# Loads in two holds, identity products, repacked FFN weights and a new order of the work, in a fused attention and FFN layer

## The chip, the cores and the metric

One core of one Trainium2 chip. The metric is the device time of an execution in microseconds. The core has five engines with instruction queues of their own, each in order: TensorE (PE in the profile; its weight loads are PEld), VectorE (DVE), ScalarE (ACT), GpSimd (POOL) and SyncE (SP, which here only issues DMAs). They meet through semaphores. Everything is float32, except three helper tiles of the quantisation.

## The reference

For 2048 tokens of width 128, one layer of retention attention and one FFN, each with a residual and a LayerNorm without weights:

```python
q = (hidden_states @ Wq).reshape(b, l, NH, DQK)      # NH = 8, DQK = 16
k = (hidden_states @ Wk).reshape(b, l, NH, DQK)
v = (hidden_states @ Wv).reshape(b, l, NH, DV)       # DV = 32
q = rope(q)
k = rope(k)
...
scores = jnp.einsum('bhqd,bhkd,hqk->bhqk', q * DQK ** (-0.5), k, decay)
o = jnp.einsum('bhqk,bhkd->bhqd', scores, v)
o = jnp.transpose(o, (0, 2, 1, 3))
o = o * jax.lax.rsqrt(jnp.mean(o * o, axis=-1, keepdims=True) + EPS) * g_norm_w
g = hidden_states @ Wg
o = o.reshape(b, l, VDIM) * (g * jax.nn.sigmoid(g))
return o @ Wo
...
gate = fp4_linear(x, w_gate)                         # 128 -> 352
y = fp4_linear(x, w_up)
h = jax.nn.silu(gate) * y
return fp4_linear(h, w_down)                         # 352 -> 128
...
x = _layernorm(x + attention(x))
x = _layernorm(x + ffn(x))
```

`fp4_linear` rounds both the activations and the weights, in blocks of 16 along the contracted axis, to the 8 magnitudes of FP4 times the block's largest magnitude over 6. The decay is causal and exponential in the distance, so the attention can be carried from chunk to chunk as a state.

## The kernel before, in words

The tokens are cut into 16 chunks of 128. For a chunk c the kernel computes, in this order of dependence:

- TensorE project_qk, then VectorE rotate (three products with tables of cosines and sines) and GpSimd rotate_add; TensorE transpose_qk; ScalarE q_even, q_odd and k_transposed (kT);
- TensorE project_vg, ScalarE v_sb and silu_g (copy_v_and_silu);
- TensorE scores, four banks of PSUM. VectorE masks the two heads of the first bank (mask_scores); ScalarE copies the other six (raw) and GpSimd masks them;
- TensorE from_state, state_product and values; VectorE next_state, which carries the state S; ScalarE copy_oT, TensorE transpose_o, ScalarE squares, VectorE mean_square (ms) and gated, GpSimd rms_rstd (rstd_h) and gated_output (y), TensorE transpose_y, ScalarE copy_yT, TensorE out_projection;
- VectorE ln1_sum, ln1_stats, ln1_aggr, ln1_eps; GpSimd ln1_rstd; ScalarE ln1_centre and ln1_norm, which writes x1 (x_blocks in the profile);
- the activation's rounding: VectorE x_amax, x_inv, x_ratio, ScalarE magic_x, VectorE x_plus, x_grid, GpSimd x_value; TensorE transpose_xq, ScalarE copy_xqT, TensorE gate and up, ScalarE silu_of_gate, VectorE h_product;
- the same rounding of the 352-wide h (h_amax to h_value), TensorE transpose_h, ScalarE copy_hT, TensorE down; VectorE ln2_sum, ln2_stats, ln2_aggr, ln2_eps, GpSimd ln2_rstd, ScalarE ln2_norm, and a store of 64 KB by SP.

Each engine's queue is a loop over stages s, written out by hand. In a stage, `run(f, a)` issues operation f of chunk s + a if there is such a chunk. The lists of these lines, one for each engine, and their numbers a set the whole order; nothing else schedules. A "stage" of the prediction is one turn of TensorE's loop. The eight banks of PSUM have several users each (scores, oT, o and yT in banks 0 to 3; QK and its transposes in 4; VG and the output projection in 5; gate, xqT and hT in 6; up, down and the state product U in 7), and TensorE waits for the last user's reader before it fills a bank again.

Before they can be used, the FFN's weights are rounded too, once, on VectorE and ScalarE between the first chunks (weights_amax, weights_inv, weights_ratio, weights_magic, weights_plus, weights_grid, weights_value; number 0 is gate and up, wgu, number 1 is down, wd). TensorE transposes them in stages 2 and 3. `scale_wo` folds the norm's weight into Wo.

Chunks are loaded in groups (chunk 0; 1 and 2; 3 to 7; 8 to 15), each as x transposed, tables and x for the residual. SP issues all loads one after the other, without a wait, and then the 16 stores, each behind a wait for its ln2_norm. ScalarE issues w_vg, the masks and the three other weights before its first work.

## Time and profile before

| | us |
|---|---|
| median of 3 runs | 147.26 (146.16 to 148.52) |
| the profiled execution | 146.5 |
| its span, first to last instruction | 144.8 |
| TensorE busy | 118.7 (82%) |
| VectorE busy | 115.6 (80%) |
| ScalarE busy | 96.0 (66%) |
| GpSimd busy | 101.6 (70%) |

Busy shares are means over the span, in which stages with different limits follow each other; the views by stretch below tell more. Times inside the profile count from the span's start. An instruction's duration in the profile overlaps the next one's start a little when the queue is full. A wait is put down to the engine or DMA that came last.

### The profile page before, as it was taken

The numbers are of one execution on the slowest core, as the hardware profiler recorded it, in microseconds if no ns is written. First come the engines' busy times: TensorE is split into PE (matmuls) and PEld (weight loads), VectorE is DVE, ScalarE is ACT, GpSimd is POOL, SyncE is SP. The second block draws the span as 40 slices with busy tenths as digits, with TensorE's granted clock in tenths as the row PEclk, the third lists the DMA queues.
The fourth block names the chain that finished last, engine by engine and source line by source line (L and its number), as shares of the span: only waits on it lengthen the run. The fifth ranks groups of instructions, "written<-read, shape, count | busy, mean of one in ns | idle before, by whom it ended". The sixth has DMA issues, their size and how long they took to land.

```text
span 144.8 us, 3493 instructions
## 1 busy us (share of the span) xinstructions
PE 118.7 (82%) x1206; PEld 74.1 (51%) x1206; DVE 115.6 (80%) x438; ACT 96.0 (66%) x279; POOL 101.6 (70%) x139
## 2 busy tenths in 40 slices
PE   0339779889999999999999999999999787767600
PEld 0123344636666465675756676666667453435400
DVE  1086979497589999989898989899899999979420
ACT  1316647697877977969595868787788575533680
POOL 4010494786978899879797979898989877464830
PEclk9999999999999999999999999999999999999985
DMA  3999960000000000000000000000000000000143
GB/s 115 243 382 374 440 194 0 0 2 7 0 0 5 0 0 7 0 2 5 0 0 5 0 2 0 5 2 5 0 0 5 0 0 0 2 0 0 37 146 109
DMA packets 6404, 7.57 MB, mean 52 GB/s; under 512 B 667, under 2 KB 5531, under 8 KB 6259
## 3 DMA queue, kind: packets, MB, share of 16 engines
q1 hardware_dynamic: 5712, 6.42, 13.1%
q10 hardware_dynamic: 675, 0.94, 2.1%
q8 instruction: 9, 0.15, 0.4%
q14 instruction: 8, 0.07, 0.2%
HBM read 6.31 MB, written 1.05 MB: 51 GB/s over the span
## 4 chain that ended last, share of the span: by engine, by line
PE 67%; DVE 10%; ACT 6%; POOL 6%; DMA 4%; issue 2%; SPq 1%; ACTq 0%
PE ps L319 9%; PE ps L336 6%; PE ps L460 6%; PE ps L437 6%; PE ps L444 5%; PE ps L376 5%; PE ps L312 5%; DMA tabs<-rope_tables 4%; PE ps L451 4%; PE ps L366 4%; PE ps L400 3%; PE ps L349 2%; PE ps L401 2%; POOL rstd_h L872 2%; ACT x L490 2%
## 5 line engine op out<-in xcount | busy, mean ns | idle before, releaser
L872 POOL TENSOR_TENSOR rstd_h<-ms,minus_half 128x8 f32<-128x8 f32 x16 | 26.3, 1645 | 8.6 <-DVE ms L726 8.2
L883 POOL TENSOR_TENSOR rstd<-veps,minus_half 128x1 f32<-128x1 f32 x32 | 18.7, 594 | 2.1 <-DVE veps L742 2.0
L319 PE MATMUL ps<-w_vg,xT 128*128 128x512 f32 x32 | 18.0, 646 | 0.1
L460 PE MATMUL ps<-wd_T,hT 128*128 128x128 f32 x96 | 14.1, 283 | 4.3 <-DVE h_blocks L779 2.3
L867 POOL TENSOR_SCALAR_AFFINE_SELECT probs<-raw 128x768 f32<-128x768 f32 x16 | 13.9, 866 | 5.1 <-ACT raw L489 4.9
L863 POOL TENSOR_TENSOR qk<-rope_c,rope_s 128x256 f32<-128x256 f32 x16 | 11.7, 730 | 6.4 <-DVE rope_s L703 6.4
L460 PEld LDWEIGHTS ps<-wd_T,hT 128*128 128x128 f32 x96 | 12.5, 191 | 7.2 <-DVE h_blocks L779 4.2
L890 POOL TENSOR_TENSOR xq<-x_grid,xs 128x128 f32<-128x128 f32 x16 | 9.1, 571 | 9.6 <-DVE x_grid L642 9.6
L312 PE MATMUL ps<-w_qk,xT 128*128 128x256 f32 x32 | 11.8, 453 | 4.8 <-DMA w_qk<-in_w_qk 4.8
L896 POOL TENSOR_TENSOR hq<-h_grid,hs 128x352 f32<-128x352 f32 x16 | 12.9, 809 | 3.7 <-DVE h_grid L642 3.7
L489 ACT ACTIVATE raw<-ps 128x768 f32<-128x768 f32 x16 | 13.1, 816 | 1.0 <-PE ps L336 0.8
L490 ACT ACTIVATE q_eo<-ps,consts 128x128 f32<-128x128 f32 x32 | 9.9, 365 | 5.7 <-PE ps L328 5.7
L565 ACT ACTIVATE silu_h<-ps 128x352 f32<-128x352 f32 x16 | 7.4, 463 | 7.9 <-PE ps L437 7.7
L489 ACT ACTIVATE oT<-ps 128x256 f32<-128x256 f32 x16 | 6.2, 384 | 9.5 <-PE ps L376 9.5
L701 DVE TENSOR_TENSOR rope_c<-ps,tabs 128x256 f32<-128x256 f32 x16 | 6.7, 419 | 7.0 <-DMA tabs<-rope_tables 6.4
L336 PE MATMUL ps<-q_eo,kT 32*128 32x256 f32 x128 | 12.1, 444 | 0.2 <-ACT kT L490 0.2
L444 PE MATMUL ps<-wgu_T,xqT 128*128 128x352 f32 x32 | 12.1, 460 | 0.0
L437 PE MATMUL ps<-wgu_T,xqT 128*128 128x352 f32 x32 | 12.1, 460 | 0.0
L489 ACT ACTIVATE hT<-ps 128x384 f32<-128x384 f32 x16 | 7.9, 496 | 4.9 <-PE ps L451 4.8
L877 POOL TENSOR_TENSOR y<-gate_o,rstd_h 128x256 f32<-128x256 f32 x16 | 9.9, 617 | 1.3
L376 PE MATMUL ps<-probs,v_sb 128*32 128x128 f32 x256 | 10.4, 273 | 0.4 <-POOL probs L867 0.4
L451 PE MATMUL ps<-ident,hq 128*128 128x128 f32 x48 | 8.7, 290 | 2.0 <-ACT silu_h L565 1.8
(99 smaller groups left out, 337.4 us busy)
## 6 DMA issues: line engine op xcount, KB each, us to landing
tabs<-rope_tables SPq DMA_DIRECT2D x1, 1536.0 KB, 12.3
out<-x SPq DMA_DIRECT2D x16, 64.0 KB, 1.6
tabs<-rope_tables SPq DMA_DIRECT2D x1, 960.0 KB, 8.7
xT<-x_transposed SPq DMA_DIRECT2D x1, 512.0 KB, 9.3
x_res<-x SPq DMA_DIRECT2D x1, 512.0 KB, 13.4
tabs<-rope_tables SPq DMA_DIRECT2D x1, 384.0 KB, 7.0
wgu_nat<-in_w_gate_up ACTq DMA_DIRECT2D x1, 352.0 KB
xT<-x_transposed SPq DMA_DIRECT2D x1, 320.0 KB, 6.8
```

The costliest lines, as they stand in the source:

```text
L312: mm(qk_ps, xT[:, c * C:(c + 1) * C], w_qk[:], start=True, stop=True).then_inc(qk_pe, 1)
L319: mm(vg_ps, xT[:, c * C:(c + 1) * C], w_vg[:], start=True, stop=True).then_inc(vg_pe, 1)
L336: last = mm(sc_ps(j), kT[rows, c % D, :], q_eo[rows, c % D, :, :].rearrange("p e q -> p (e q)"), start=True, stop=True)
L376: last = mm(oT_ps[32 * slot32:32 * slot32 + 32, n // 4, :], v_sb[:, c % D, n * DV:(n + 1) * DV], probs[:, c % 2, n, :], start=c == 0, stop ...
L437: mm(gate_ps, xqT[:, c % 2, :], wgu_T[:, 0, :], start=True, stop=True).then_inc(gate_pe, 1)
L444: mm(up_ps, xqT[:, c % 2, :], wgu_T[:, 1, :], start=True, stop=True).then_inc(up_pe, 1)
L451: last = transpose(hT_ps[:, t * C:(t + 1) * C], hq[:, c % 2, t * 128:(t + 1) * 128], ident[:])
L460: last = mm(down_ps, hT[:, c % 2, t, :], wd_T[:, t, :], start=t == 0, stop=t == 2)
L489: copy = lambda o, i: nc.scalar.activation(o, i, ACT.Copy)
L867: gp.affine_select(out=probs[:, c % 2, 2 * MB:, :], in_=raw[:, c % 2, :, :], compare_op=ALU.is_ge, fill=0.0, base=0, pattern=[[0, NH - 2 * ...
L872: gp.tensor_tensor(rstd_h[:, c, :], ms[:, c, :], minus_half[:], ALU.pow).then_inc(rms_p, 1)
L883: gp.tensor_tensor(rstd[n][:, c, :], veps[n][:, c, :], minus_half[:, 0:1], ALU.pow).then_inc(ln_p[n], 1)
```

## The change

The tables lose a third: the sines were stored twice, once negated, and the negation is now made by a `scalar_tensor_tensor` in rotate, so a chunk's tables are 128 KB instead of 192 KB. The gate and up weights, 88 rows of 1024 elements before, lie on all 128 partitions with 704 elements each (`WG`), and are loaded by five DMAs instead of one and transposed in other pieces. SP waits after x and tables of chunk 0 until these tables have landed, and again before the last group. w_qk moves from SP to the head of ScalarE's queue, w_down and Wo from ScalarE to SP; the weights of gate and up are issued after ScalarE's first activation. TensorE gets four identity products at its start and four after chunk 0's project_qk. The lists of all four compute engines are written in another order and with other numbers; the loops have 33 stages instead of 38.

```diff
-WR = 88
+WR = I
 WT = I // WR
+WG = 2 * I * H // 128
...
-        FIRST, LAST = -3, 35
+        FIRST, LAST = -4, 29
...
             load_x(0)
-            sp.dma_start(w_qk[:], wqk).then_inc(d_wqk, 16)
             load_tables(0)
+            sp.wait_ge(d_tab[0], 16)
             load_x(1)
             load_tables(1)
+            sp.dma_start(wd_nat[:], w_down).then_inc(d_wd, 16)
+            sp.dma_start(wo_nat[:], wo_g).then_inc(d_wo, 16)
             load_res(0)
             load_res(1)
             load_x(2)
             load_tables(2)
             load_res(2)
+            sp.wait_ge(d_tab[1], 16)
             load_x(3)
             load_tables(3)
             load_res(3)
...
+            def warm_up(n):
+                pe.wait_ge(c_ident, 1)
+                for _ in range(n):
+                    mm(ps[:, 7, 0:C], ident[:], ident[:], start=True, stop=True)
...
                 fill(4, "qk")
+                if c == 0:
+                    warm_up(4)
...
+            act_engine.dma_start(w_qk[:], wqk).then_inc(d_wqk, 16)
             act_engine.dma_start(w_vg[:], wvg).then_inc(d_wvg, 16)
             act_engine.dma_start(consts[:], cst).then_inc(d_cst, 16)
-            act_engine.dma_start(wgu_nat[:], w_gate_up).then_inc(d_wgu, 16)
-            act_engine.dma_start(wd_nat[:], w_down).then_inc(d_wd, 16)
-            act_engine.dma_start(wo_nat[:], wo_g).then_inc(d_wo, 16)
             act.wait_ge(c_pool, 4)
             nc.scalar.activation(table_io[:], minus_half[:], ACT.Silu)
+            act_engine.dma_start(wgu_nat[:, 0:4 * H].rearrange("p (t n) -> p t n", n=2 * H),
+                                 w_gate_up[0:2 * H, :].rearrange("(t p) n -> p t n", p=H)).then_inc(d_wgu, 16)
+            act_engine.dma_start(wgu_nat[0:96, 4 * H:5 * H], w_gate_up[2 * H:I, 0:H]).then_inc(d_wgu, 16)
+            act_engine.dma_start(wgu_nat[96:128, 4 * H:5 * H], w_gate_up[2 * H:288, H:]).then_inc(d_wgu, 16)
+            for m in range(2):
+                act_engine.dma_start(wgu_nat[m * 64:(m + 1) * 64, 5 * H:],
+                                     w_gate_up[288:I, H + m * 64:H + (m + 1) * 64]).then_inc(d_wgu, 16)
...
-                dve.wait_ge((d_wgu, d_wd)[n], 16)
+                dve.wait_ge((d_wgu, d_wd)[n], (80, 16)[n])
...
-                for e in range(2):
-                    vec.tensor_tensor(g16(rope_s[:, c % D, :])[:, :, e, :], g16(qk_ps)[:, :, 1 - e, :],
-                                      g16(tabs[:, c, H:])[:, :, e, :], ALU.mult).then_inc(rope_v, 1)
+                sin = tabs(c)[:, H:].rearrange("p (g f) -> p g f", f=16)
+                vec.scalar_tensor_tensor(g16(rope_s[:, c % D, :])[:, :, 0, :], g16(qk_ps)[:, :, 1, :], -1.0, sin,
+                                         ALU.mult, ALU.mult).then_inc(rope_v, 1)
+                vec.tensor_tensor(g16(rope_s[:, c % D, :])[:, :, 1, :], g16(qk_ps)[:, :, 0, :], sin, ALU.mult).then_inc(
+                    rope_v, 1)
...
-                run(ln2_norm, -19)
...
+                run(ln2_norm, -13)
...
-                run(down, -7)
-                run(gate, -3)
...
+                run(down, -8)
+                run(gate, -4)
```

What the new lists do shows in three places. First, VectorE at the program's start, from behind its memsets (L701, L703 or L726 to L730 rotate, wr_small the weights' maxima and scales, probs the mask). Before:

```order
L701 TENSOR_TENSOR rope_c<-ps,tabs 128x256 [waits qk_pe,d_tab0]
L703 TENSOR_TENSOR rope_s<-ps,tabs 128x8x16 x2
L625 TENSOR_REDUCE wr_small<-wgu_nat 88x64 [waits d_wgu]
L659 TENSOR_SCALAR wr_small<-wr_small 88x64 [waits w0_amax_v]
L661 RECIPROCAL wr_small<-wr_small 88x64 [waits w0_amax_v]
L662 TENSOR_SCALAR wr_small<-wr_small 88x64
L633 SCALAR_TENSOR_TENSOR wr_ratio<-wgu_nat,wr_small 88x1024 [waits w0_inv_v]
L625 TENSOR_REDUCE wr_small<-wd_nat 128x22 [waits d_wd]
L709 TENSOR_TENSOR probs<-ps,causal 128x256 [waits sc_pe,c_ident]
```

and now:

```order
L726 TENSOR_TENSOR rope_c<-ps,tabs_sb 128x256 [waits qk_pe,d_tab0]
L728 SCALAR_TENSOR_TENSOR rope_s<-ps,tabs_sb 128x8x16
L730 TENSOR_TENSOR rope_s<-ps,tabs_sb 128x8x16
L650 TENSOR_REDUCE wr_small<-wgu_nat 128x44 [waits d_wgu]
L650 TENSOR_REDUCE wr_small<-wd_nat 128x22 [waits d_wd]
L684 TENSOR_SCALAR wr_small<-wr_small 128x22 [waits w1_amax_v]
L686 RECIPROCAL wr_small<-wr_small 128x22 [waits w1_amax_v]
L687 TENSOR_SCALAR wr_small<-wr_small 128x22
L736 TENSOR_TENSOR probs<-ps,causal 128x256 [waits sc_pe,c_ident]
L684 TENSOR_SCALAR wr_small<-wr_small 128x44 [waits w0_amax_v]
L686 RECIPROCAL wr_small<-wr_small 128x44 [waits w0_amax_v]
L687 TENSOR_SCALAR wr_small<-wr_small 128x44
```

The large ratio of the gate and up weights has left the stretch ahead of the first mask. Both waits for weight DMAs still stand there, and the DMAs they wait for are issued later.

Second, TensorE in a stage in which every operation has a chunk, from the value products on (L376 or L392 values, L451 transpose_h, L400 and L401 or L416 and L417 out_projection, L384 and L385 or L400 and L401 transpose_o, L444 or L464 up, L319 or L335 project_vg, L429 or L449 transpose_xq, L336 or L352 scores, L457 gate, L480 down). Before:

```order
L376 MATMUL ps<-probs,v_sb 32x128 x8
L451 MATMUL ps<-ident,hq 128x128 x3
L400 MATMUL ps<-wo_s,yT 128x128
L401 MATMUL ps<-wo_s,yT 128x128
L384 MATMUL ps<-ident,oT 128x128
L385 MATMUL ps<-ident,oT 128x128
L327 MATMUL ps<-ident,qk 128x128
L328 MATMUL ps<-ident,qk 128x128
L444 MATMUL ps<-wgu_T,xqT 128x352
L319 MATMUL ps<-w_vg,xT 128x512
L429 MATMUL ps<-ident,xq 128x128
L336 MATMUL ps<-q_eo,kT 128x256 x4
```

and now:

```order
L392 MATMUL ps<-probs,v_sb 32x128 x8
L449 MATMUL ps<-ident,xq 128x128
L416 MATMUL ps<-wo_s,yT 128x128
L417 MATMUL ps<-wo_s,yT 128x128
L400 MATMUL ps<-ident,oT 128x128
L401 MATMUL ps<-ident,oT 128x128
L343 MATMUL ps<-ident,qk 128x128
L344 MATMUL ps<-ident,qk 128x128
L480 MATMUL ps<-wd_T,hT 128x128 x3
L457 MATMUL ps<-wgu_T,xqT 128x352
L335 MATMUL ps<-w_vg,xT_sb 128x512
L352 MATMUL ps<-q_eo,kT 128x256 x4
```

transpose_xq has come ahead of the output projection and transpose_h has left the place; down and gate stand between transpose_qk and project_vg, where up stood alone.

Third, ScalarE at the end of the program (x<-r,rstd is ln2_norm, hT the copy of the transposed h). Before:

```order
L502 ACTIVATE h_magic<-h_ratio 128x352
L490 ACTIVATE x<-r,rstd 128x128
L489 ACTIVATE hT<-ps 128x384
L490 ACTIVATE x<-r,rstd 128x128
L489 ACTIVATE hT<-ps 128x384
L490 ACTIVATE x<-r,rstd 128x128 x14
```

and now:

```order
L528 ACTIVATE h_magic<-h_ratio 128x352
L511 ACTIVATE x<-r,rstd 128x128
L510 ACTIVATE hT<-ps 128x384
L511 ACTIVATE x<-r,rstd 128x128
L510 ACTIVATE hT<-ps 128x384
L511 ACTIVATE x<-r,rstd 128x128 x7
```

Seven of the final normalisations, instead of fourteen, stand behind the last copy of hT.

## Rows read from the trace of the kernel before

**Rows 1.** The page, part 2: GB/s in each of 40 slices of 3.62 us.

```profile
GB/s 115 243 382 374 440 194 0 0 2 7 0 0 5 0 0 7 0 2 5 0 0 5 0 2 0 5 2 5 0 0 5 0 0 0 2 0 0 37 146 109
```

**Rows 2.** Stretches: start and end; length, then busy time of PE, PEld, DVE, ACT, POOL.

```profile
34.60:40.70 6.10, 6.10 (x73) 4.00 (x72) 3.90 (x17) 5.01 (x16) 5.01 (x7) 1.00 0.02 4
...
72.40:79.20 6.80, 6.80 (x77) 4.49 (x76) 6.31 (x27) 5.22 (x17) 5.62 (x8) 1.00 0.01 2
...
112.60:118.00 5.40, 4.26 (x22) 2.50 (x21) 5.26 (x23) 3.95 (x11) 4.74 (x7) 1.00 0.00 0
```

**Rows 3.** Timeline of the start: start, duration in us, instruction, idle before and releaser.

```profile
1.24 0.42 SPq L235 DMA_DIRECT2D w_qk<-in_w_qk  x1
...
1.71 0.42 SPq L226 DMA_DIRECT2D tabs<-rope_tables  x1
...
3.24 1.28 ACT L498 ACT_TABLE_LOAD   x1 [3.24 <-issue]
...
4.79 1.22 PE L312 MATMUL ps<-w_qk,xT 128*128 128x256 f32 x2 [4.79 <-DMA w_qk<-in_w_qk]
...
7.89 0.43 DVE L701 TENSOR_TENSOR rope_c<-ps,tabs 128x256 f32<-128x256 f32 x1 [6.44 <-DMA tabs<-rope_tables]
...
8.62 1.21 DVE L625 TENSOR_REDUCE wr_small<-wgu_nat 88x64 f32<-88x1024 f32 x1
...
13.33 0.42 DVE L709 TENSOR_TENSOR probs<-ps,causal 128x256 f32<-128x256 f32 x1 [1.01 <-PE ps L336]
...
17.13 0.43 DVE L726 TENSOR_REDUCE ms<-o_sq 128x8 f32<-128x264 f32 x1 [0.15 <-ACT o_sq L549]
```

**Rows 4.** DMA issues: tile, queue, KB each, median us from issue to landing.

```profile
w_vg<-in_w_vg ACTq DMA_DIRECT2D x1, 256.0 KB, 3.2
tabs<-rope_tables SPq DMA_DIRECT2D x1, 192.0 KB, 6.2
wd_nat<-in_w_down ACTq DMA_DIRECT2D x1, 176.0 KB, 6.5
...
w_qk<-in_w_qk SPq DMA_DIRECT2D x1, 128.0 KB, 3.5
...
xT<-x_transposed SPq DMA_DIRECT2D x1, 64.0 KB, 2.9
```

**Rows 5.** Chain of waits: start, duration, what; project_vg of three chunks.

```profile
10.32 1.71 PE ps L319 x2
...
35.31 0.86 PE ps L319 x2
...
72.95 0.95 PE ps L319 x2
```

**Rows 6.** Chain of waits: values of chunks 1 and 2, rstd_h between, down.

```profile
21.17 0.44 PE ps L376 x16
...
23.51 1.68 POOL rstd_h L872
...
27.05 0.44 PE ps L376 x16
...
68.46 0.67 PE ps L460 x6
```

**Rows 7.** Timeline of the last microseconds: SP's stores and the last variance.

```profile
138.01 5.17 SPq L249 DMA_DIRECT2D out<-x  x11
...
138.31 0.15 DVE L742 TENSOR_SCALAR veps<-mv 128x1 f32<-128x1 f32 x1
```

**Rows 8.** Waits: who waited for whom, us in total, times, longest.

```profile
PEld ps L336 <- ACT kT L490: 7.7, 15, 1.5
```

**Rows 9.** Timeline of VectorE in a full stage.

```profile
77.94 0.52 DVE L642 SCALAR_TENSOR_TENSOR h_grid<-h_magic,h_plus 128x352 f32<-128x352 bf16 x1
...
78.38 0.28 DVE L642 SCALAR_TENSOR_TENSOR x_grid<-x_magic,x_plus 128x128 f32<-128x128 bf16 x1
...
78.58 0.52 DVE L633 SCALAR_TENSOR_TENSOR h_ratio<-h_blocks,hs 128x352 f32<-128x352 f32 x1
```

More of the change, by code:

```diff
@@ L311, in project_qk @@
                 free_qk_bank()
-                mm(qk_ps, xT[:, c * C:(c + 1) * C], w_qk[:], start=True, stop=True).then_inc(qk_pe, 1)
+                mm(qk_ps, xT(c), w_qk[:], start=True, stop=True).then_inc(qk_pe, 1)
                 fill(4, "qk")
+                if c == 0:
+                    warm_up(4)
             def project_vg(c):
@@ L318, in project_vg @@
                 free_vg_bank()
-                mm(vg_ps, xT[:, c * C:(c + 1) * C], w_vg[:], start=True, stop=True).then_inc(vg_pe, 1)
+                mm(vg_ps, xT(c), w_vg[:], start=True, stop=True).then_inc(vg_pe, 1)
                 fill(5, "vg")
@@ L408, in transpose_gate_up_weights @@
                 free_up_bank()
-                for m, dst in enumerate((gate_ps, up_ps)):
-                    for t in range(WT):
-                        k = (m * WT + t) * H
-                        last = transpose(dst[:, t * WR:(t + 1) * WR], wgu_q[:, k:k + H], ident[0:WR, 0:WR])
+                for t in range(2):
+                    for m, dst in enumerate((gate_ps, up_ps)):
+                        k = (2 * t + m) * H
+                        transpose(dst[:, t * H:(t + 1) * H], wgu_q[:, k:k + H], ident[:])
+                transpose(gate_ps[:, 2 * H:I], wgu_q[0:96, 4 * H:5 * H], ident[0:96, 0:96])
+                transpose(up_ps[:, 2 * H:288], wgu_q[96:128, 4 * H:5 * H], ident[96:128, 96:128])
+                for half in (slice(0, 64), slice(64, 128)):
+                    last = mm(ps[half, 7, 288:I], wgu_q[half, 5 * H:], ident[half, half], start=True, stop=True)
                 last.then_inc(wT_pe, 1)
@@ L462, in down @@
                 fill(7, "down")
+            warm_up(4)
             for s in range(FIRST, LAST):
                 run = stage_runner(s)
+                run(state_product, 0)
+                run(values, 0)
+                run(transpose_xq, -4)
+                run(out_projection, -1)
                 run(transpose_o, 0)
                 run(transpose_qk, 1)
-                run(up, -4)
+                run(down, -8)
+                run(gate, -4)
+                run(project_vg, 1)
+                run(scores, 1)
                 if s == 3:
@@ L472, in _ @@
                     transpose_gate_up_weights()
-                run(project_vg, 1)
-                run(transpose_xq, -3)
-                run(scores, 1)
+                run(up, -4)
+                run(transpose_h, -7)
                 run(project_qk, 2)
-                run(down, -7)
-                run(gate, -3)
                 run(transpose_y, 0)
                 run(from_state, 1)
-                run(state_product, 1)
-                run(values, 1)
-                run(transpose_h, -6)
-                run(out_projection, 0)
         @block.scalar
@@ L806, in _ @@
                     weights_grid(1)
-                if s == -1:
-                    scale_wo()
+                run(ln1_sum, 1)
+                run(h_inv, -3)
+                run(mean_square, 2)
+                run(gated, 2)
+                if s == 1:
+                    weights_value(1)
+                if s == -3:
+                    weights_amax(0)
+                run(x_amax, 0)
+                run(ln2_sum, -6)
+                if s == -3:
+                    weights_amax(1)
+                run(x_plus_, -1)
@@ L812, in _ @@
-                run(ln1_eps, 0)
-                run(rotate, 3)
-                run(h_amax, -3)
+                run(mask_scores, 3)
+                run(h_product, -2)
+                if s == -3:
+                    weights_inv(0)
+                run(ln2_eps, -7)
+                run(ln1_aggr, 1)
+                run(x_inv, 0)
+                run(rotate, 4)
                 if s == -2:
                     weights_plus(0)
-                run(ln2_sum, -6)
-                run(h_inv, -3)
-                run(next_state, 2)
@@ L820, in _ @@
-                run(x_plus_, -1)
-                if s == 1:
-                    weights_value(1)
-                run(h_grid_, -4)
-                if s == -1:
-                    weights_inv(1)
-                run(x_grid_, -1)
-                run(h_ratio_, -3)
-                run(ln2_eps, -7)
-                run(ln2_stats, -6)
-                if s == -1:
-                    weights_ratio(1)
-                run(ln1_sum, 1)
-                run(x_amax, 0)
-                run(mean_square, 2)
@@ L835, in _ @@
-                if s == -3:
-                    weights_amax(0)
-                if s == -3:
-                    weights_inv(0)
-                run(ln1_stats, 1)
-                if s == -3:
-                    weights_ratio(0)
+                run(ln2_stats, -6)
+                run(ln1_eps, 1)
+                run(h_amax, -2)
+                run(next_state, 3)
+                if s == -1:
+                    weights_value(0)
+                run(ln2_aggr, -6)
+                if s == -3:
+                    scale_wo()
```

115 lines of the change are left out of this document (57 added, 58 removed).

## The prediction

> **What bounds the kernel now.** I read the table of stages first, then the timeline of each end, the DMA issues, and last the chain of waits. The stages differ [rows 2]: from about 28 to 112 us TensorE is full (6.10 of 6.10, 6.80 of 6.80), in stages of 5.9 us before the FFN's down product has joined and of 6.8 behind it. From 112 us VectorE is full (5.26 of 5.40) and TensorE has holes. Two stretches have neither full: the first 14 us, and the last 6.
>
> Start [rows 3]: chunk 0's QK product runs at 4.79 us, when w_qk has landed, but rotate(0) waits until 7.89 for its 192 KB of tables, issued at 1.71. They took 6.2 us to land, against 2.9 and 3.5 for the transfers issued just before them [rows 4]: they share the DMA engines with everything behind. VectorE then does weight work, and masks chunk 0 at 13.33 us, after 1.01 us of waiting for the scores.
>
> End [rows 7]: the last chunk's variance is ready at 138.46 us (138.31 + 0.15), but 11 of the 16 stores are issued between 138.01 and 143.18 us, 0.47 each, and the span ends at 144.8. The stores, bunched behind 14 normalisations, are the bound there.
>
> **The change, part by part.**
>
> *First loads.* SP now issues x(0) and tables(0), and nothing else until the tables have landed. The tables are 128 KB, w_qk's old size in w_qk's old place, so I take its 3.5 us from 1.24: landed at 4.75. w_qk goes first on ACT's queue, where 256 KB of w_vg took 3.2 us from 0.80: landed by 4.0. QK(0) then runs from 4.0 to 5.0, its old length being 1.22, and rotate(0) starts at 5.0 instead of 7.89: **2.9 us earlier**. Its three instructions keep their widths and cost nothing new; the third of the tables that is dropped (1 MB) relieves later transfers, which no row waits for.
>
> *Weights in VectorE's way.* Behind rotate(0) VectorE now meets both weight maxima and the inverse of the down weights, before mask(0) and rotate(1). Queued behind the DMA waits are thus the mask that chunk 0's values need, and all of chunk 1. wgu is five ACT DMAs behind the table load (which took 1.28 us and can start at about 2.2, as two DMAs now leave ACT's queue ahead of it): from 3.75 us, about 0.45 each, to 6.1. w_down is third on SP after the release, issued at 5.75. Between 4.85 us and its landing some 900 KB must move (x 128, tables 256, w_down 176, wgu 352), at the 243 to 382 GB/s of the page's slices two and three [rows 1]: 2.4 to 3.8 us, and about 2 us that a small transfer takes over its bytes (64 KB took 2.9). So it lands between 9.0 and 10.9; by its old 6.5 us, 12.2. I take 9.6, near the lower end, because the old 6.5 had three times the bytes in flight. The maxima cost 1.21 x 704/1024 = 0.83 and 0.5 us, the inverse chain 0.5: mask(0) starts near 11.0 instead of 13.33. Then 0.4 for the mask and 2.3 for the small scales, rotate(1), the state and scale_wo: ms(0) starts at 13.75 instead of 17.13. **Start: 3.4 us earlier**, between 0.3 (w_down at 12.2, less what is hidden) and 4.0.
>
> The trace has a small transfer landing 2.9 us after its issue, and each hold exposes that once, here between 1.24 and 7.8 us for chunk 1's x. The Trainium skill (DMA: Bandwidth & Descriptors, on the two cost components) speaks against holding loads on a completion in the same way, with about 2.0 us fixed plus the bytes over 436 GB/s; by it alone all 900 KB are in at 4.85 + 2.0 + 2.1 = 9.0, an estimate, and the sum would be 0.4 lower.
>
> *Identity products.* Four stand before QK(0) and four behind it, on an idle TensorE; the second four delay nothing, since transpose_qk(0) waits for GpSimd's addition until about 6.7 us. They may change the clock. VG(0)'s two passes took 1.71 us, a later chunk's 0.86 [rows 5]: 1.2 against 2.4 GHz, although the profile's granted clock says 1.00 in both stretches. With TensorE active from 1.9 us, VG and scores may save about 1.4 us in all; but mask(0) waits for the weights by then, so I count **zero**. If that cover goes (weights by 9.0), at most 0.4 of it is seen.
>
> *ACT.* The magic of the down weights (0.5 us) now stands before the copy of chunk 1's scores, for which transpose_y(0) and GpSimd's mask wait: **+0.4**. That of the gate and up weights is covered by the wait for y.
>
> *Filling.* Until TensorE is full, a stage is a loop of 5.88 us: values, oT, squares, ms, rstd (1.68 us on GpSimd), y, its transpose, values [rows 6]. The order of these links is kept. transpose_xq now lies between values and transpose_o: 0.2 us in three stages, **+0.6**. gate, up and transpose_xq, and down too, begin a stage later: the stage that ends at values(8) loses down's 0.67, the one at values(4) 0.15, being near the loop's floor: **-0.8**.
>
> *Steady state.* TensorE keeps its instructions and the number of changes between tile shapes. VG's 0.86 us were 0.95 in a full stage [rows 5], as it waited for VectorE's ln1_sum; down and gate now lie between the two, and that goes: seven stages, **-0.6**. What is late next is the copy of kT, waited for in 15 stages already [rows 8]; it has 0.55 us ahead of it (x_blocks, x_magic), where it had hT's 0.5. VectorE (6.31 of 6.80) and GpSimd (5.62) keep their work and stay under.
>
> *Drain.* Behind mean_square(15) VectorE's new order has more left: one h_grid and h_ratio, and one each of x_amax, x_plus, x_grid, ln2_sum and ln2_stats. In a full queue the next start comes 0.44 us after an h-wide one and 0.20 after an x-wide one [rows 9]: 2 x 0.44 + 5 x 0.20 = **+1.9**. In the last stages down follows up and transpose_h instead of leading them, one hT copy more before ln2_sum: **+0.4**.
>
> *Stores.* Only 7 normalisations are left behind the last copy of hT. From the last variance: rstd 0.6, norm 0.4, then the store, 0.47 of issue and 1.6 to the end, together 3.1 us instead of 6.3: **-3.2**. Seven stores need 3.3 us of SP and start 3 us before: hidden.
>
> **Sum:** -3.4 + 0.4 + 0.6 - 0.8 - 0.6 + 1.9 + 0.4 - 3.2 = -4.7: span 140.1. Around the span the profiled execution has 1.7 us (146.5), so 141.8 against its own time. The median of the runs shown is 0.8 above that execution, within their spread (146.16 to 148.52); I go half way: **142.2**.
>
> **Rivals.**
>
> 1. *Weights late.* If the last of them lands at 12.2 us, 3.1 of the start's 3.4 are lost: 145.3. For: w_down took 6.5 us, and wgu's pieces have rows of 256 to 1024 bytes. Against: far less is in flight. Chance 0.10.
>
> 2. *A link slips by 0.2 us in every full stage.* Four engines' orders changed at once; thirteen stages give +2.6: 144.8. Against: VectorE has 0.5 us of room in a stage. Chance 0.14.
>
> 3. *Slower: kT closes a loop.* ACT is in order, and x_blocks waits for GpSimd's rstd, which stands behind mask, x_value and rotate_add. Place: kT before each chunk's scores. By a walk from start to start kT is ready some 0.25 us before the scores are due. From a slip of 0.6 us (0.38 a stage over thirteen) the kernel is slower than before; at 0.9, 0.65 a stage is +8.5: 150.7. For: the scores wait for kT already, by up to 1.5 us in one stage. Against: ACT is busy 5.22 of 6.80. Chance 0.08.
>
> 4. *The clock stays low or falls back.* TensorE waits some 2 us for mask(0). With chunk 0's and 1's products at double time, +1: 143.2, inside the forecast. The Trainium skill (TensorE: Matmul & The Clock Gate, what you observe) has the throttled state as the default and activity as what releases it; the passes of rows 5 agree with two levels, and no row shows what identity products do.
>
> 5. *Better than forecast:* weights by 9.0 and a shorter drain, 138.5 or below. Chance 0.06.
>
> **Numbers.** Forecast (138.5 to 143.9) 0.62, rivals 1, 2, 3, 5 as given. About 2% is what a measurement can tell from no change: under 144.3 is faster, over 150.2 slower. Faster: 0.62, 0.06 and a quarter of rivals 1 and 2, 0.74. Slower: most of rival 3, and what I have not seen, 0.07. Same: 0.19. The range 138.5 to 145.5 leaves out rival 3, the better case and the upper tail of 2.
>
> **What would show it.** rotate(0) at 5 us; VectorE idle before the maxima until 9 to 10 for a DMA; mask(0) near 11, ms(0) near 13.8; a full stage of 6.7 to 6.8 with no wait of VG; values(15) about 4 us earlier than now; the last variance near 137; the last store directly behind the last normalisation. The forecast falls if weights arrive after 12 us, if a full stage takes over 7.0, or if ACT's stall before the scores of chunk 1 comes back in later chunks.

## The result: 139.8 us, 5.1% faster

| | before | after |
|---|---|---|
| median of 4 runs, us | 147.59 (146.16 to 148.52) | 139.80 (139.24 to 141.37) |
| ratio, 95% interval | | 0.9485 (0.9399 to 0.9571) |
| span of the profiled execution | 144.8 | 137.5 |
| time of the profiled execution | 146.5 | 140.22 |

The ratio is of the fast runs alone, without the 148.52 and 141.37 us, and so differs a little from that of the two medians.

The forecast of 142.2 us (138.5 to 145.5) had the direction and held the time, and was 2.4 us short in size. First the page after; its lines are busy time, share of the span and instructions.

```profile
PE 121.0 (88%) x1224; PEld 77.9 (57%) x1224; DVE 115.8 (84%) x438; ACT 97.3 (71%) x279; POOL 102.9 (75%) x139
```

Every engine is busy 0.2 to 2.3 us longer than before: none got less work, and the 7.3 us of span are holes. To see where they were, I took the start of mean_square (ms) on VectorE, the link that every chunk has once, from both timelines:

| start, us | ms(0) | ms(6) | ms(8) | ms(15) | last h_product | last ln2_sum | span |
|---|---|---|---|---|---|---|---|
| before | 17.13 | 52.85 | 66.01 | 113.01 | 129.80 | 137.44 | 144.8 |
| after | 13.02 | 48.95 | 61.03 | 107.99 | 125.43 | 133.32 | 137.5 |
| earlier by | 4.11 | 3.90 | 4.98 | 5.02 | 4.37 | 4.12 | 7.3 |

So 4.1 us come from the start, 0.2 go back while the pipeline fills, 1.1 come from the stages in which down used to join, 0.9 go back in the drain, and 3.2 come from the stores. The timeline of the start (start, duration, instruction, idle before and releaser), beside [rows 3]:

```profile
1.91 2.07 PE L320 MATMUL ps<-ident 128*128 128x128 f32 x8 [1.91 <-POOL ident L879]
...
2.21 1.28 ACT L517 ACT_TABLE_LOAD   x1 [2.21 <-issue]
2.28 0.39 ACTq L518 DMA_DIRECT2D wgu_nat<-in_w_gate_up  x1
...
4.95 0.42 DVE L726 TENSOR_TENSOR rope_c<-ps,tabs_sb 128x256 f32<-128x256 f32 x1 [3.50 <-PE ps L326]
...
7.11 1.26 PE L335 MATMUL ps<-w_vg,xT_sb 128*128 128x512 f32 x2
...
7.71 0.89 DVE L650 TENSOR_REDUCE wr_small<-wgu_nat 128x44 f32<-128x704 f32 x1 [1.95 <-DMA wgu_nat<-in_w_gate_up]
...
8.76 0.52 DVE L650 TENSOR_REDUCE wr_small<-wd_nat 128x22 f32<-128x352 f32 x1 [0.16 <-DMA wd_nat<-in_w_down]
...
9.00 0.70 PE L326 MATMUL ps<-w_qk,xT_sb 128*128 128x256 f32 x2
...
9.76 0.41 DVE L736 TENSOR_TENSOR probs<-ps,causal 128x256 f32<-128x256 f32 x1
...
13.02 0.41 DVE L753 TENSOR_REDUCE ms<-o_sq 128x8 f32<-128x264 f32 x1
...
13.28 1.02 PE L335 MATMUL ps<-w_vg,xT_sb 128*128 128x512 f32 x2
```

rotate(0) starts at 4.95, forecast 5.0, and waits for TensorE, no longer for the tables. The first weight DMA is issued at 2.28, while ScalarE's table load runs until 3.49; I had put it behind the load, at 3.75. So both weights are there by 8.76 instead of 9.6, and mask(0) starts at 9.76. Chunk 0's VG takes 1.26 us, against 1.91 in the timeline of before (1.71 in [rows 5], which counts only its part of the chain).

The 1.1 us between ms(6) and ms(8) are TensorE's. In windows from the one to the other (length, then busy time of PE, PEld, DVE, ACT, POOL, and the granted clock) it was full before:

```profile
52.85:66.01 13.16, 13.07 (x148) 8.36 (x147) 12.41 (x47) 10.44 (x33) 11.46 (x15) 1.00 0.01 2
```

and has 1.11 us less to do after:

```profile
48.95:61.03 12.08, 11.96 (x141) 7.53 (x140) 11.90 (x45) 10.14 (x32) 10.76 (x14) 1.00 0.01 4
```

That work isn't gone. The FFN's products of a chunk come a stage later, and at the other end TensorE has 1.06 us more to do between ms(15) and the last h_product (13.82 us instead of 12.76, below), where it has holes. No experiment undoes the order of work in the middle; this is read from the two traces.

Next, VectorE in the drain, from ms(15) to the last h_product, with the same columns. Before:

```profile
113.01:129.80 16.79, 12.76 (x63) 7.42 (x62) 15.86 (x64) 9.31 (x26) 11.25 (x16) 1.00 0.00 0
```

and after, with a full stage ahead of it:

```profile
65.90:72.70 6.80, 6.80 (x88) 4.57 (x81) 6.52 (x28) 5.50 (x17) 5.81 (x7) 1.00 0.00 0
107.99:125.43 17.44, 13.82 (x70) 8.38 (x70) 17.30 (x69) 11.02 (x32) 12.18 (x18) 1.00 0.05 16
```

VectorE has 1.44 us more to do in the drain, but 0.93 us of it was idle before and 0.14 is now: only 0.65 us of length came of it. The tail, the answer to [rows 7]:

```profile
132.55 3.34 SPq L256 DMA_DIRECT2D out<-x  x7
...
133.32 0.29 DVE L784 TENSOR_TENSOR r<-ps,x_blocks 128x128 f32<-128x128 f32 x1 [1.10 <-PE ps L480]
...
134.19 0.15 DVE L769 TENSOR_SCALAR veps<-mv 128x1 f32<-128x1 f32 x1
...
135.07 0.40 ACT L511 ACTIVATE x<-r,rstd 128x128 f32<-128x128 f32 x1 [0.27 <-POOL rstd L910]
```

Seven stores are left and the last follows the last normalisation; the span ends 3.2 us behind the variance at 134.34 (134.19 + 0.15). From the last ln2_sum to the end it is 4.2 us, against 7.4 before. Last, the wait that answers to [rows 8]:

```profile
PEld ps L352 <- ACT kT L511: 13.7, 16, 1.2
```

It has grown from 7.7 to 13.7 us. Whether it costs anything is for an experiment.

### The profile page after: what moved, and what is told of

It reads as the page before. It is cut to its first block, busy times and chain, and to the rows that moved or that the text cites. A ratio compares the mean times of both kernels' runs of the same rounds, so it can differ in the third digit from the quotient of the medians.

```text
span 137.5 us, 3532 instructions
## 1 busy us (share of the span) xinstructions
PE 121.0 (88%) x1224; PEld 77.9 (57%) x1224; DVE 115.8 (84%) x438; ACT 97.3 (71%) x279; POOL 102.9 (75%) x139
## 3 DMA queue, kind: packets, MB, share of 16 engines
q10 hardware_dynamic: 1024, 0.76, 1.7%
HBM read 5.26 MB, written 1.05 MB: 46 GB/s over the span
## 4 chain that ended last, share of the span: by engine, by line
PE 65%; ACT 12%; DVE 8%; DMA 5%; POOL 4%; issue 3%; SPq 1%; POOLq 0%; DVEq 0%; ACTq 0%
PE ps L464 7%; PE ps L480 7%; PE ps L352 6%; PE ps L392 5%; PE ps L335 4%; PE ps L382 4%; PE ps L326 4%; PE ps L457 3%; PE ps L471 3%; PE ps L416 3%; ACT q_eo L511 3%; PE ps L417 3%; DMA wd_nat<-in_w_down 3%; PE ps L365 3%; PE ps L449 3%
## 5 line engine op out<-in xcount | busy, mean ns | idle before, releaser
L923 POOL TENSOR_TENSOR hq<-h_grid,hs 128x352 f32<-128x352 f32 x16 | 15.0, 935 | 2.9 <-DVE h_grid L667 2.9
L335 PE MATMUL ps<-w_vg,xT_sb 128*128 128x512 f32 x32 | 16.9, 610 | 0.1
L480 PE MATMUL ps<-wd_T,hT 128*128 128x128 f32 x96 | 13.6, 278 | 2.7 <-ACT hT L510 2.7
L464 PE MATMUL ps<-wgu_T,xqT 128*128 128x352 f32 x32 | 13.7, 510 | 1.1 <-DVE r L784 1.1
L480 PEld LDWEIGHTS ps<-wd_T,hT 128*128 128x128 f32 x96 | 12.1, 193 | 3.5 <-DVE r L784 2.6
L352 PEld LDWEIGHTS ps<-q_eo,kT 32*128 32x128 f32 x128 | 5.0, 183 | 13.7 <-ACT kT L511 13.7
L352 PE MATMUL ps<-q_eo,kT 32*128 32x256 f32 x128 | 11.4, 426 | 0.9 <-ACT kT L511 0.6
L457 PE MATMUL ps<-wgu_T,xqT 128*128 128x352 f32 x32 | 12.2, 464 | 0.0
L904 POOL TENSOR_TENSOR y<-gate_o,rstd_h 128x256 f32<-128x256 f32 x16 | 10.8, 674 | 1.3
L726 DVE TENSOR_TENSOR rope_c<-ps,tabs_sb 128x256 f32<-128x256 f32 x16 | 6.6, 414 | 5.7 <-PE ps L326 5.5
L392 PE MATMUL ps<-probs,v_sb 128*32 128x128 f32 x256 | 10.6, 274 | 0.2 <-POOL probs L894 0.2
L574 ACT ACTIVATE o_sq<-ps 128x256 f32<-128x256 f32 x16 | 6.1, 384 | 6.5 <-PE ps L401 6.5
L806 DVE TENSOR_TENSOR h_blocks<-ps,silu_h 128x352 f32<-128x352 f32 x16 | 8.3, 522 | 2.5 <-PE ps L464 2.4
L326 PE MATMUL ps<-w_qk,xT_sb 128*128 128x256 f32 x32 | 10.4, 409 | 0.0
```

The costliest lines, as they stand in the source:

```text
L326: mm(qk_ps, xT(c), w_qk[:], start=True, stop=True).then_inc(qk_pe, 1)
L335: mm(vg_ps, xT(c), w_vg[:], start=True, stop=True).then_inc(vg_pe, 1)
L352: last = mm(sc_ps(j), kT[rows, c % D, :], q_eo[rows, c % D, :, :].rearrange("p e q -> p (e q)"), start=True, stop=True)
L392: last = mm(oT_ps[32 * slot32:32 * slot32 + 32, n // 4, :], v_sb[:, c % D, n * DV:(n + 1) * DV], probs[:, c % 2, n, :], start=c == 0, stop ...
L457: mm(gate_ps, xqT[:, c % 2, :], wgu_T[:, 0:I], start=True, stop=True).then_inc(gate_pe, 1)
L464: mm(up_ps, xqT[:, c % 2, :], wgu_T[:, I:2 * I], start=True, stop=True).then_inc(up_pe, 1)
```

## The experiments

All twelve were timed in three rounds beside the kernel before; the ratios below are to it. Kernels named a_ and c_ are edits of the changed kernel, those named b_ of the one before. In the first group one step is undone, or done alone.

**The stores.** In a_norm19 ln2_norm goes back to its old number, in b_norm13 the old kernel gets the new one.

```diff
-        FIRST, LAST = -4, 29
+        FIRST, LAST = -4, 35
...
-                run(ln2_norm, -13)
+                run(ln2_norm, -19)
```

> The changed kernel with ln2_norm back at 19 stages behind (and 35 as the last stage), all else kept. Theory 1: from the last variance to the end takes 6.3 us again instead of 3.3, since 14 normalisations and 11 stores are left; the last variance itself stays at 134.3 us within 0.3. So span 140.7 (+3.2), about 142.7 us as a run, 0.967 of the kernel before. Rival: the new order of the other engines hides the stores anyway, and the end moves by under 1 us; then the 3.2 us came from elsewhere.

> The kernel before with ln2_norm 13 stages behind instead of 19, nothing else. Theory 1: the stores are worth the same 3.2 us alone: span 141.6, ratio 0.978. Rival: ScalarE's normalisations, now inside the drain's stages, are in the way of hT and h_magic there, and the last variance comes later than 138.5 by 1 us or more: ratio 0.985 or above.

Measured: a_norm19 143.96 us, ratio 0.9799 (0.9718 to 0.9880); b_norm13 145.20, 0.9830 (0.9723 to 0.9937). SP's stores of a_norm19:

```profile
132.37 6.16 SPq L256 DMA_DIRECT2D out<-x  x13
```

and the last ones of b_norm13:

```profile
138.05 3.65 SPq L249 DMA_DIRECT2D out<-x  x8
```

With the old number 13 stores are issued in one row again, to 138.5. From the last ln2_sum to the end it is 6.96 us in a_norm19 and 4.58 in b_norm13: this one number is worth 2.8 us, whichever kernel it stands in, and its cost in the drain is at most 0.3 (17.05 instead of 16.79 us in b_norm13, 17.44 in a_norm19 as in after). The medians are further apart in the changed kernel: a_norm19's is 4.2 us above after's and 1.3 above what was expected. Some 0.5 of the 4.2 lies around the span; its spans are 140.1, 140.8, 141.6 and 141.6 us, so the profiled execution is the shortest, and what the others had besides the stores is open.

In b_norm13 rotate(0) started at 8.96, and in b_fill below at 9.01, instead of 7.89 [rows 3], both waiting for the tables: the kernel before varies by 1.1 us in that DMA, which rotate(0) no longer waits for. So the profiled execution of before was probably one with early tables; that would be most of the 1.5 us by which the medians of before and after (7.8 us) differ by more than their profiled executions do (6.3).

**The identity products.** a_no_warm drops both calls.

```diff
-                if c == 0:
-                    warm_up(4)
...
-            warm_up(4)
```

> The changed kernel without the eight identity products. Theory (clock is hidden): VG(0)'s two passes take 1.7 us instead of 1.26 and scores(0) 1.2 instead of 0.65, so scores(0) end near 10.0 us instead of 9.0 and mask(0) starts at 10.1 instead of 9.76; ms(0) then comes 0.3 to 0.8 us later, ratio to the changed kernel 1.002 to 1.006. Rival A: no effect at all, the passes are as fast without them. Rival B: the low clock lasts into chunk 1 and costs over 1.5 us (141.5 or more).

Measured: 140.00 us, 0.9519 (0.9470 to 0.9568). TensorE in its timeline:

```profile
6.88 1.92 PE L333 MATMUL ps<-w_vg,xT_sb 128*128 128x512 f32 x2
8.73 1.24 PE L350 MATMUL ps<-q_eo,kT 32*128 32x256 f32 x8
9.90 1.22 PE L326 MATMUL ps<-w_qk,xT_sb 128*128 128x256 f32 x2
11.05 0.44 PE L363 MATMUL ps<-v_sb,qk 128*32 128x64 f32 x8
11.26 1.54 PE L390 MATMUL ps<-probs,v_sb 128*32 128x128 f32 x16
```

Everything up to 12.8 us takes about twice its later time, as at 1.2 instead of 2.4 GHz, and TensorE goes through without a hole: the mask, ready at 10.1 + 0.4, is no longer what values(0) wait for. QK(1) is, which stands between scores(0) and them. ms(0) starts at 14.24 instead of 13.02: the identity products are worth 1.2 us there, more than the 0.3 to 0.8 expected. These are single executions: in the profiles of the other a_ kernels that keep the products, the holds and the order at the start, ms(0) starts between 12.78 and 13.49, so the gain lies between 0.75 and 1.5. The first four products also cost something: QK(0) starts at 3.77 behind them and at 3.32 without, rotate(0) at 4.95 and 4.66. VectorE's wait for the weights hides that. Of the gain, 0.7 us are left in the medians of the spans (137.55 and 138.25) and 0.2 in those of the times, as two of after's executions have 2.7 us around the span and a_no_warm's all 1.7. What takes the rest, the next run shows.

**The changed kernel again**, as the control of a later group (a_same; an empty line is the only difference).

> The changed kernel again, unchanged, as the control of this call. 139.8 us median before (139.24 to 141.37). Clock theory: TensorE's raised clock falls back in some executions in the quiet stretch from 9.7 to 13 us (project_vg of chunk 1 took 1.02 us in three of the profiled variants and 1.9 in two), so the runs spread over about 1.5 us. Rival: the spread comes from the landing of the weights alone; then project_vg(1) has no part in it.

Measured: 140.67 us (139.88 to 141.37), 0.9554 (0.9482 to 0.9626). TensorE in its timeline, the same instructions as after's at 13 us:

```profile
12.92 0.41 PE L344 MATMUL ps<-ident,qk 128*128 128x128 f32 x1
13.12 1.92 PE L335 MATMUL ps<-w_vg,xT_sb 128*128 128x512 f32 x2
14.97 1.24 PE L352 MATMUL ps<-q_eo,kT 32*128 32x256 f32 x8
```

and two stretches of it, the granted clock being the third number from the end:

```profile
9.40:13.10 3.70, 1.98 (x29) 1.16 (x29) 3.63 (x13) 1.06 (x3) 1.59 (x2) 0.98 0.92 190
13.10:15.10 2.00, 2.00 (x8) 0.50 (x6) 1.66 (x4) 0.91 (x4) 1.75 (x2) 0.50 1.05 359
```

The clock has fallen to 0.50, the 1.2 GHz level, after a stretch in which TensorE worked for 1.98 of 3.70 us, and ms(1) starts 1.0 us later than after's. The profile of after has the same 1.98 of 3.70 and keeps 1.00, so with this load it goes either way. The spans of a_same are 137.4, 138.5, 138.7 and 138.8 us; those of after 137.5, 137.5, 137.6 and 138.7; of a_no_warm, whose TensorE is busy for 3.40 us of that stretch, 138.2 to 138.5, and its profile keeps 1.00. The products gain 1.2 us, and in some executions the clock takes 1.0 to 1.3 back. The slow VG(1), 1.92 us, stands in the profiles of a_same, a_no_hold and a_fill; in those of after, a_norm19 and a_kt_first it takes 1.02. That executions without a profile differ by the same fall is inferred from their spans.

**The holds.** a_no_hold drops both of SP's waits.

```diff
             load_tables(0)
-            sp.wait_ge(d_tab[0], 16)
...
-            sp.wait_ge(d_tab[1], 16)
```

> The changed kernel without SP's two waits (for tables 0 and tables 1); the order of the DMAs stays. Theory: tables(0) share the engines with all that follows and land after 6 to 7 us instead of 4.35 (they took 6.2 us from their issue before, with 192 KB; with 128 KB I expect 4.5 to 5.5), so rotate(0) starts at 5.8 to 6.8 instead of 4.95; weights land at about the same time, so that half of it is hidden behind the weights' maxima: +0.3 to +1.5 us in the time. Rival: the holds do nothing, tables and w_qk come first because they are issued first: rotate(0) at 5.0, no difference.

Measured: 141.90 us, 0.9619 (0.9540 to 0.9697). VectorE in its timeline:

```profile
4.96 0.42 DVE L724 TENSOR_TENSOR rope_c<-ps,tabs_sb 128x256 f32<-128x256 f32 x1 [3.51 <-PE ps L324]
...
9.33 0.89 DVE L648 TENSOR_REDUCE wr_small<-wgu_nat 128x44 f32<-128x704 f32 x1 [3.56 <-DMA wgu_nat<-in_w_gate_up]
...
11.12 0.41 DVE L734 TENSOR_TENSOR probs<-ps,causal 128x256 f32<-128x256 f32 x1
```

The theory's mechanism failed. The tables need no hold: they land in 3.1 us with it and without. Their size isn't the reason either, for in b_loads (below) the old 192 KB, in the same place and with the hold, land in 3.3 us, against 6.2 in the kernel before:

```profile
tabs<-rope_tables SPq DMA_DIRECT2D x1, 192.0 KB, 3.3
```

What the holds protect is the weights. The DMA issues of after (KB each, us from issue to landing):

```profile
wgu_nat<-in_w_gate_up ACTq DMA_DIRECT2D x1, 256.0 KB, 2.9
...
wd_nat<-in_w_down SPq DMA_DIRECT2D x1, 176.0 KB, 3.5
```

and of a_no_hold:

```profile
wgu_nat<-in_w_gate_up ACTq DMA_DIRECT2D x1, 256.0 KB, 4.7
wd_nat<-in_w_down SPq DMA_DIRECT2D x1, 176.0 KB, 5.5
```

So mask(0) is 1.36 us later (11.12 against 9.76) and ms(0) 0.8; the clock fell in this execution too, which adds the rest of the 2.0 in span. In the medians it is 2.1 us (141.90 against 139.80), more than the 1.5 expected. Which of the two waits brings it was not separated. The Trainium skill (DMA: Bandwidth & Descriptors, on the two cost components) prices a transfer by itself, as a fixed part and a part by its bytes; that this speaks against a hold was the prediction's reading, and it isn't borne out. Such a sum has no term for what a transfer gains when others are held back, here 1.8 and 2.0 us for the weights, while the fixed part that the hold exposes is covered by other waits.

**The loads alone, in the kernel before.** b_loads takes the order of the DMAs and the holds, with the old tables and 88-row weights in one DMA; b_loads_warm adds the identity products.

```diff
             load_x(0)
-            sp.dma_start(w_qk[:], wqk).then_inc(d_wqk, 16)
             load_tables(0)
+            sp.wait_ge(d_tab[0], 16)
...
+            act_engine.dma_start(w_qk[:], wqk).then_inc(d_wqk, 16)
             act_engine.dma_start(w_vg[:], wvg).then_inc(d_wvg, 16)
```

> The kernel before with the new loads alone: w_qk at the head of ScalarE's queue, wgu (one DMA, 88 rows as before) behind the first activation's issue, w_down and Wo on SP, both holds; tables still 192 KB, old order of work, old weights. Theory: rotate(0) starts at 5.0 to 5.5 instead of 7.89, but VectorE's 3.7 us of weight work on 88 rows stands behind it and waits for wgu, so mask(0) starts at 11.0 to 11.8 instead of 13.33: ms(0) 1.5 to 2.3 us earlier, ratio 0.985 to 0.990. Rival: all 2.9 us come through to ms(0), ratio 0.980; then the repacked weights and their new place on VectorE bring nothing at the start.

> b_loads (the kernel before with the new loads alone, where ms(0) started at 14.07 us) with the eight identity products. Theory: loads and clock make the whole gain of the start, the repacked weights and VectorE's new order nothing: project_vg(0) 1.0 to 1.3 us instead of 1.91, ms(0) at 12.8 to 13.3, as in the changed kernel (13.02). Rival: VectorE's chain of weight work on 88 rows (to 10.8 us before mask(0)) is the bound once TensorE is faster, and ms(0) stays at 13.6 or later.

Measured: b_loads 144.27 us, 0.9776 (0.9699 to 0.9853), and b_loads_warm 144.17, 0.9785 (0.9666 to 0.9903). VectorE of b_loads_warm:

```profile
7.20 1.22 DVE L635 TENSOR_REDUCE wr_small<-wgu_nat 88x64 f32<-88x1024 f32 x1 [1.44 <-DMA wgu_nat<-in_w_gate_up]
...
9.26 1.22 DVE L643 SCALAR_TENSOR_TENSOR wr_ratio<-wgu_nat,wr_small 88x1024 f32<-88x1024 f32 x1
...
10.83 0.41 DVE L719 TENSOR_TENSOR probs<-ps,causal 128x256 f32<-128x256 f32 x1
...
13.51 0.43 DVE L736 TENSOR_REDUCE ms<-o_sq 128x8 f32<-128x264 f32 x1 [0.22 <-ACT o_sq L559]
```

ms(0) starts at 14.07 in b_loads, 3.06 earlier than before: the order of the loads and the holds alone bring three quarters of the start. With the identity products it is 13.51, and TensorE then waits 1.52 us for the mask, behind VectorE's long chain over 88 rows; mask(0) starts at 10.83, and at 9.76 in after. The other 0.5 us, from 13.51 to 13.02, fit the repacked weights and their new place, but aren't shown to be theirs: a_fill, which has both, also started ms(0) at 13.49 in its profile, and the rest between 12.78 and 13.11. Without the identity products nothing of them is seen (a_no_warm 14.24, b_loads 14.07). In the medians b_loads and b_loads_warm are not told apart. In the profiled execution of b_loads the last microseconds are odd:

```profile
131.00:136.00 5.00, 3.73 (x15) 3.09 (x15) 1.61 (x9) 3.00 (x10) 2.94 (x6) 0.57 0.17 50
```

The clock fell in the drain; the last two downs took 1.47 and 1.62 us instead of 0.91, and 1.6 of the 3.04 us still there at ms(15) were gone at the last ln2_sum.

**kT first.** a_kt_first copies kT ahead of x1's normalisation.

```diff
+                run(k_transposed, 3)
                 run(ln1_norm, 0)
                 run(magic_x, -1)
-                run(k_transposed, 3)
```

> The changed kernel with k_transposed moved on ScalarE ahead of ln1_norm and magic_x (directly behind q_odd). Theory A (the chain of waits names q_eo, x_blocks and kT in five filling stages of 5.89 us): each gets 0.4 to 0.5 us shorter, 2 to 2.5 us in all, 137.5. Theory B (two loops of the same length: ms to values takes 4.06 us in those stages, as it did before the change): scores come 0.5 us earlier, but transpose_y still waits for y; at most 0.3 us per kernel, 139.5 within 0.6, the waits for kT halved.

Measured: 139.19 us, 0.9449 (0.9372 to 0.9525). Its waits for the scores:

```profile
PEld ps L352 <- ACT kT L511: 7.3, 9, 1.0
...
PEld ps L352 <- issue: 5.3, 7, 0.8
```

kT is early now in seven stages, and in each the weight load stands idle nearly as long as before: it is behind VG's 1.02 us of matmul then, and TensorE (PE) is busy for 40.00 us of 40.00 (65 to 105 us) in either kernel. From ms(1) to ms(15) it takes 88.56 us instead of 88.90, and c_best against c_warm, below, gives the same (88.59 and 88.93). So some 0.3 of the 13.7 us cost time; the rest was idle time of the weight loads, not of the bound.

**VectorE in the drain.** a_fill and b_fill add one 128x352 product to a tile that nobody reads, behind h_product, in four stages of the drain.

```diff
+                if s in (13, 14, 15, 16):
+                    vec.scalar_tensor_tensor(scratch[:], wd_nat[:], 1.0, wd_nat[:], ALU.mult, ALU.mult)
```

> The changed kernel with one additional product of 352 elements per partition (0.44 us in a full queue) on VectorE in each of the four stages before h_product of chunk 15; it writes an unused tile. Theory: VectorE is the bound there (17.29 busy of 17.40 us), so the last variance and the end come 1.6 to 1.8 us later: 141.5. Rival: the drain is a loop between TensorE and VectorE with room in it, under 0.8 us later.

> The kernel before with the same four additional products in the four stages before its h_product of chunk 15. Theory: here VectorE had 0.94 us of idle time between mean_square(15) and h_product(15) (15.86 busy of 16.80), which takes up a part: 0.8 to 1.3 us later, against 1.6 to 1.8 in the changed kernel. That is why the drain cost 0.65 us there and not the 1.9 forecast. Rival: 1.7 us later here too; then the idle time was not free, and the forecast's count of work was wrong instead.

Measured: a_fill 142.73 us, 0.9664 (0.9575 to 0.9752); b_fill 148.50, 1.0069 (1.0019 to 1.0119). ms(15) to the last h_product in a_fill:

```profile
109.31:129.45 20.14, 14.25 (x70) 8.63 (x70) 20.05 (x74) 11.12 (x32) 12.76 (x18) 1.00 0.05 14
```

and in b_fill:

```profile
114.59:132.46 17.87, 12.84 (x63) 7.42 (x62) 17.67 (x68) 9.75 (x26) 11.15 (x15) 1.00 0.00 0
```

From the start of each product to the next instruction, the four took 2.94 us in a_fill and 2.07 in b_fill; the drains grew by 2.70 and 1.08. The expected 1.6 to 1.8 for a_fill was too little, since it priced each product by 0.44 us and two of them held VectorE for 0.95 beside GpSimd's work; b_fill came within its 0.8 to 1.3. After the change VectorE is the bound of the drain nearly throughout (0.92 of what is added comes through); before, 1.0 us fitted into its holes. That is where most of my +1.9 went wrong.

**Better versions.** c_warm adds identity products in the quiet stretch, behind QK(1) and behind values(0). c_best has these too, kT first, the inverse of the gate and up weights behind rotate(1), and the copy of the scores ahead of the down weights' magic.

```diff
                 if c == 0:
                     warm_up(4)
+                if c == 1:
+                    warm_up(2, 6)
...
+                if c == 0:
+                    warm_up(2, 6)
```

> The changed kernel with four more identity products: two behind project_qk(1), two behind values(0), into bank 6. Clock theory: no execution falls back; project_vg(1) at 1.0 to 1.1 us, median 0 to 0.6 us under the control's and the slowest run no more than 0.8 us above the fastest. If it is false: the same spread as the control, and up to 0.3 us more for the products in front of transpose_o(0).

> c_warm, and k_transposed ahead of ln1_norm and magic_x, the small scales of the gate and up weights behind rotate(1), and the magic of the down weights behind the copy of chunk 1's scores. Theory: 0.3 us from kT in the middle (span 137.0 against 137.5 in the look at it), and 0.3 to 0.5 us at the start, since rotate(1) begins at 10.2 instead of 11.3 and transpose_y(0) no longer waits for raw: span 136.5 to 136.9, about 0.8 us under the control. Rival: GpSimd's mask of chunk 1, behind y(0), is the floor there, and the start gives nothing.

Measured, in one group with a_same: c_warm 139.32 us (139.12 to 140.21), 0.9475 (0.9411 to 0.9540); c_best 139.01 (138.59 to 139.98), 0.9452 (0.9383 to 0.9522). TensorE in c_warm:

```profile
9.29 0.61 PE L320 MATMUL ps<-ident 128*128 128x128 f32 x4
...
11.25 0.71 PE L320 MATMUL ps<-ident 128*128 128x128 f32 x4
...
13.03 1.02 PE L337 MATMUL ps<-w_vg,xT_sb 128*128 128x512 f32 x2
```

VG(1) has the full clock in the profiles of both c_warm and c_best. That proves little, as three of six profiles without the additional products had it too, and nothing says that it held in all eight executions; their spans, 136.8 to 138.5 us, fit that, once 1.2 us of another kind are known. SP's line of stores in c_warm gives the shortest, median and longest issue in ns:

```profile
L256 SPq DMA_DIRECT2D out<-x x16: 332/338/1757, 103.3 to 136.5; - x16
```

One issue took 1.76 us and held the stores behind it, so this span ends 5.4 us after the last ln2_sum at 133.13, not 4.2; c_best's has one of 1.68. Whether the new order at the start gave anything in c_best stays open: rotate(1) starts at 10.46 (c_warm 11.09), but ms(1) at 18.93 (18.84). The rival names GpSimd as the floor, and transpose_y(0) does wait 0.86 us for y there. But the gate and up weights also came 0.4 us later in this execution (their maximum starts at 8.13, in c_warm at 7.73), and mask(0) with them. c_best has the lowest median of all, 1.7 us under its control and 0.8 under after's; its interval overlaps a_kt_first's, c_warm's, after's and a_same's, so this order among them isn't shown. Part of it lies around the span: the medians of the spans are 137.15 us in c_best, 137.55 in c_warm and in after, and 138.6 in a_same.

## Why the prediction was right, and what it got wrong

The direction, the two large gains and their causes were right. The pieces between were off by up to 1.25 us: 3.2 us too dear in all (start, filling, down, drain), 0.6 too cheap in the full stages, and the range was wide enough for the 2.6 that remain. The table sets the forecast's terms beside the measured ones; -0.15 of the -0.8 was meant for a stage before ms(6).

| step | forecast | measured, between |
|---|---|---|
| start, to ms(0) | -3.4 | -4.1 |
| ACT's magic, transpose_xq (to ms(6)) | +1.0 | +0.2 |
| down a stage later (to ms(8)) | -0.8 | -1.1 |
| full stages (to ms(15)) | -0.6 | 0.0 |
| drain, VectorE (to the last h_product) | +1.9 | +0.65 |
| down behind up (to the last ln2_sum) | +0.4 | +0.25 |
| stores | -3.2 | -3.2 |
| span | -4.7 | -7.3 |

- **Start.** Right in its mechanism: rotate(0) at 4.95, the weights next. Two sizes were off. The weights came 0.8 us sooner, being issued beside the table load: gate and up were in flight from 2.28, and so didn't belong among the 900 KB still to move from 4.85. (The sum for them was also short in its fixed part: 64 KB in 2.9 us leave 2.6 to 2.7 over the bytes at those rates, not 2, which would have put the landing at 9.9 to 11.3.) And "*I count zero*" for the identity products was the mis-sized term: they measured 1.2 us. I had looked only at VG and scores, which lie ahead of the mask; QK(1), the state product and the values stand behind them on the same queue and ran at the low clock too, with no cover. Against that, mask(0) to ms(0) took 3.26 us and not 2.75: two VectorE instructions took 0.84 and 0.85 us (below).
- **Filling.** The 0.6 for transpose_xq and 0.4 for the magic were charged as if both lay on the path; together 0.2 was seen, all of it between ms(0) and ms(1) (6.06 us instead of 5.87). transpose_y(0) did wait for raw, 0.38 us. The gain from down's later entry came where it was put, a little larger: all that left TensorE there, 1.11 us, came off a stretch in which it was full.
- **Full stages.** ms(8) to ms(14) takes 40.64 us instead of 40.96, half of the 0.6; five of the six stages are 6.76 us, 6.83 before. That VG's wait was what went is not shown apart. kT's wait grew as the prediction named it, without a price; the last stage gave 0.3 back as VectorE filled up.
- **Drain.** The step that failed most, by 1.25 us. It priced seven instructions by a full queue. The trace has six more between ms(15) and the last h_product (the ln2_stats isn't among them), with 1.44 us of busy time: 0.45 of the miss is that. The other 0.8 is the idle time that it left out: VectorE had 0.9 us of holes there, which the window of ms(15) to h_product would have shown and the 5.4 us of [rows 2] didn't (5.26 busy of 5.40). b_fill against a_fill shows both sides.
- **Stores.** Right to 0.1 us in place, cause and size; alone it is worth 2.8.
- **Around the span**, the profiled execution after has 2.7 us and not 1.7. That isn't explained. Most executions have 1.7 or 1.8; 2.3 to 2.9 stand in two of after's, three of a_same's, three of a_no_hold's and all of a_norm19's. That the forecast took half of the 0.8 by which before's median lay over its profiled execution was a guess.

Of the rivals, *weights late* fell with the weights' landing by 8.76 us, *a link slips* with the stage of 6.76, and *kT closes a loop* with a_kt_first. *The clock falls back* came true in some executions, for 1.0 to 1.3 us, its price of 1. *Better* (138.5 or below) was reached by no median, though both its conditions came true, weights by 9.0 and a shorter drain than forecast.

## What to carry to other kernels

Price added work against the idle time of its own stretch: here the same four instructions cost 2.7 us in one order and 1.1 in the other (they took 2.9 and 2.1 on VectorE itself). A long wait in the table (13.7 us for kT) is no cost while the engine's other half is busy; move it and look at the stage. With the FFN a stage later, 1.1 us of TensorE's work left a stretch that it fills for one in which it has holes; VectorE's moved along to where VectorE is the bound, and 0.65 us of the gain went back. And look for final stores in one row behind the last result: one number in a list gave 2.8 of the 7.3 us.
